# Rotating queries and keys from the raw projections, and normalising them afterwards in place

## The reference

```python
def attn_layer(x, Wqkv, qs, ksc, Wo):
    qkv = x @ Wqkv
    q, k, v = jnp.split(qkv, 3, -1)
    q, k, v = (sh(q), sh(k), sh(v))
    q = l2norm(q) * qs
    k = l2norm(k) * ksc
    q = q * cos * scale + rotate_half(q) * sin * scale
    inv = 1.0 / scale
    k = k * cos * inv + rotate_half(k) * sin * inv
    out = local_attention(q, k, v)
    ...
    return out @ Wo
...
for i in range(DEPTH):
    x = attn_layer(shift_tokens(x), Wqkv[i], q_scale[i], k_scale[i], Wo[i]) + x
    x = ffn_layer(shift_tokens(x), ln_g[i], ln_b[i], W1[i], b1[i], W2[i], b2[i]) + x
```

## Time and profile before

| | |
|---|---|
| median of 2 runs | 4887.01 us |
| the two runs | 4892.21 and 4881.81 us |
| span of the profiled execution | 4869.5 us |
| busy share of the span: TensorE, VectorE, ScalarE, GpSimd | 78%, 79%, 51%, 49% |
| wait of GpSimd for `QN` | 1791.2 us in 192 times |
| one layer (from one L1041 at 418.95 to the same at 804.53) | 385.6 us |

### The profile page before, as it was taken

One profiled execution on the slowest core, in us unless ns is written; L12 is line 12 of the kernel. 1 busy time (PEld: TensorE's weight loads), 2 busy tenths in 40 slices (PEclk: granted clock), 3 DMA queues, 4 the chain that ended last, 5 costly groups with the idle time before them and its releaser, 6 DMA issues.

```text
span 4869.5 us, 152986 instructions
## 1 busy us (share of the span) xinstructions
PE 3785.1 (78%) x64080; PEld 2581.5 (53%) x64080; DVE 3828.5 (79%) x6082; ACT 2483.4 (51%) x3705; POOL 2389.1 (49%) x1426
## 2 busy tenths in 40 slices
PE   5887887787787787788777877877877887887887
PEld 3554554554555455456435645554554554554554
DVE  4886886896896897797448878877976886986896
ACT  3554554554554565455225545554554554553553
POOL 3663563563664564455006535544553653553552
PEclk9998899899899999888878989999988998998999
DMA  2221221221221222122002212221221221221221
GB/s 82 54 57 46 53 55 48 53 54 44 58 56 51 49 57 58 40 55 63 6 10 51 57 47 51 56 57 43 57 58 39 55 59 40 57 55 44 53 57 46
DMA packets 179337, 247.34 MB, mean 51 GB/s; under 512 B 52516, under 2 KB 75040, under 8 KB 177184
## 3 DMA queue, kind: packets, MB, share of 16 engines
q1 hardware_dynamic: 178976, 242.09, 19.6%
HBM read 39.51 MB, written 1.05 MB: 8 GB/s over the span
## 4 chain that ended last, share of the span: by engine, by line
PE 35%; POOL 18%; DVE 17%; ACT 10%; issue 8%; DVEq 7%; SPq 3%; DMA 1%; ACTq 0%; POOLq 0%
POOL V L1185 9%; PE PS L390 6%; PE PS L544 5%; POOL V L1191 5%; POOL V L1193 5%; PE PS L382 4%; PE PS L466 3%; PE PS L416 3%; DVEq L1000 3%; DVE QN L927 3%; PE PS L383 2%; PE PS L384 2%; DVEq L921 2%; PE PS L576 2%; ACT PR L743 2%
## 5 line engine op out<-in xcount | busy, mean ns | idle before, releaser
L1185 POOL TENSOR_TENSOR V<-QN,TAB 128x512 f32<-128x512 f32 x768 | 1116.7, 1485 | 1791.2 <-DVE QN L927 1791.2
L382 PE MATMUL PS<-WH,XH 128*128 128x512 f32 x1152 | 634.4, 551 | 427.8 <-DVE XL L945 338.8
L697 ACT ACTIVATE RAWQK<-PS 128x1024 f32<-128x1024 f32 x384 | 392.3, 1022 | 848.5 <-PE PS L384 808.1
L934 DVE TENSOR_TENSOR U<-QN,TAB 128x1024 f32<-128x1024 f32 x384 | 736.8, 1922 | 16.4 <-issue 15.3
L390 PE MATMUL PS<-EYE,V 128*128 128x128 f32 x3072 | 449.6, 285 | 188.0 <-POOL V L1193 107.8
L1191 POOL TENSOR_TENSOR V<-V,U 128x1024 f32<-128x1024 f32 x192 | 516.6, 2690 | 81.3 <-DVE U L934 60.8
L382 PEld LDWEIGHTS PS<-WH,XH 128*128 128x128 f32 x1152 | 241.5, 210 | 560.4 <-DVE XL L945 210.3
L1193 POOL TENSOR_TENSOR V<-V,U 128x1024 f32<-128x1024 f32 x192 | 453.6, 2362 | 140.4 <-DVE U L934 140.4
L390 PEld LDWEIGHTS PS<-EYE,V 128*128 128x128 f32 x3072 | 366.1, 147 | 276.6 <-POOL V L1193 139.8
L384 PE MATMUL PS<-WL,XH 128*128 128x512 f32 x1152 | 511.2, 444 | 0.0
L383 PE MATMUL PS<-WH,XL 128*128 128x512 f32 x1152 | 511.0, 444 | 0.0
(11 more groups left out here) (150 smaller groups left out, 6509.1 us busy)
## 6 DMA issues: line engine op xcount, KB each, us to landing
V<-VS SPq DMA_DIRECT2D x3072, 64.0 KB, 2.0
U<-wqkv SPq DMA_DIRECT2D x13, 1024.0 KB, 5.2
V<-wqkv SPq DMA_DIRECT2D x13, 512.0 KB, 6.8
WO<-wo SPq DMA_DIRECT2D x13, 512.0 KB, 3.8
W<-w SPq DMA_DIRECT2D x12, 341.0 KB
ROT<-c_rot SPq DMA_DIRECT2D x1, 2048.0 KB, 10.4
QKS<-qks SPq DMA_DIRECT2D x13, 128.0 KB, 3.7
W<-w SPq DMA_DIRECT2D x12, 114.0 KB
```

The lines of the kernel that those rows point to most:

```text
L382: pe.matmul(o, XH[:, p, :], WH[:, w], start=True, stop=False)
L934: dve.tensor_tensor(paired(U[:, k]), split(QN[:, k]), per_dim(TAB[:, 2 * k * DH:(2 * k + 1) * DH], DH), ALU.mult).then_inc((u_q, u_k)[k], 1)
L1185: ins = pool.tensor_tensor(paired(V[:, k])[:, :, :, h * half:(h + 1) * half], split(QN[:, k])[:, :, :, (1 - h) * half:(2 - h) * half], per ...
```

## The change

The product with the reciprocal norm moves behind the rotation, which it commutes with. VectorE reads the raw projection straight from the PSUM banks `RAW` for its half (`rotate`), GpSimd reads ScalarE's copy `RAWQK` for its own. The sum is multiplied in place by the reciprocal norm on VectorE (`scale_rows`) in the next step. `QN` is gone; `V` has become a double buffer `VB`. TensorE projects the keys and values only after VectorE's read of the banks (`u_q`, `u_k` in place of `cp_q`, `cp_k`), and turns `VB` after the product (`nq_ready`, `nk_ready`).

```diff
 # TensorE
-                    pe.wait_ge(cp_q, c(1))
+                    pe.wait_ge(u_q, c(1))
                     project(1, p, 0)
...
-                    pe.wait_ge(rot_q, c(0))
-                    turn_qk(0, [0])
-                    pe.wait_ge(rot_ready, c(0))
-                    turn_qk(0, [1]).then_inc(t0_ready, 1)
+                    pe.wait_ge(nq_ready, c(0))
+                    turn_qk(0, q, [0])
+                    pe.wait_ge(nk_ready, c(0))
+                    turn_qk(0, q, [1]).then_inc(t0_ready, 1)
                 if a:
-                    pe.wait_ge(cp_k, c(1))
+                    pe.wait_ge(u_k, c(1))
                     project(2, p, 0).then_inc(raw_v0, 1)
 # ScalarE
-                        act.wait_ge(qn_ready, c(0))
+                        act.wait_ge(vv_ready, c(0))
                     raw(0, raw_q, cp_q, sq_q)
 # VectorE
-                if past(i, 1):
-                    dve.wait_ge(vv_ready, c(0))
-                for k in range(2):
-                    ins = dve.tensor_tensor(QN[:, k], RAWQK[:, k], rep(RN[:, k, :], [P, HEADS, DH], 2), ALU.mult)
-                ins.then_inc(qn_ready, 1)
+
+            def scale_rows(k, q, c):
+                dve.wait_ge((rot_q, rot_ready)[k], c(0))
+                rn = RN[:, k, :].rearrange("p (r j) -> p j r", r=2).unsqueeze(3).broadcast_to([P, NP_, 2, DH])
+                v = VB[:, q, k].rearrange("p (j r) d -> p j r d", r=2)
+                dve.tensor_tensor(v, v, rn, ALU.mult).then_inc((nq_ready, nk_ready)[k], 1)
+
+            def rotate(k, i, c):
+                if k == 0:
+                    dve.wait_ge(tab_ready, c(1))
                 if past(i, 1):
+                    dve.wait_ge((rot_q, rot_ready)[k], c(0))
+                dve.wait_ge((cp_q, cp_k)[k], c(1))
+                src = PS[:, RAW:RAW + 2, :].rearrange("p r (j d) -> p r j d", d=DH)
+                dve.tensor_tensor(paired(U[:, k]), src, per_dim(TAB[:, 2 * k * DH:(2 * k + 1) * DH], DH),
                                   ALU.mult).then_inc((u_q, u_k)[k], 1)
...
                 if b:
-                    rotate(1, None)
+                    scale_rows(0, 1 - p, c)
+                if a:
+                    rotate(0, i, c)
+                if b:
+                    scale_rows(1, 1 - p, c)
...
                 if a:
+                    rotate(1, i, c)
                     sum_squares(1)
...
-                if a:
-                    if past(i, 1):
-                        dve.wait_ge(rot_ready, c(0))
-                    rotate(0, c(1))
 # GpSimd
-                pool.wait_ge(qn_ready, c(1))
-                if past(i, 1):
-                    pool.wait_ge(t1_ready, c(0))
+                if past(i, 2):
+                    pool.wait_ge(t1_ready, c(-1))
                 half = DH // 2
                 for k in range(2):
+                    pool.wait_ge((cp_q, cp_k)[k], c(1))
                     for h in range(2):
```

More of the change, by code:

```diff
@@ L121, in build @@
         TAB = sb("TAB", [P, 4 * DH])
-        QN = sb("QN", [P, 2, HEADS, DH])
         U = sb("U", [P, 2, HEADS, DH])
-        V = sb("V", [P, 2, HEADS, DH])
+        VB = sb("VB", [P, 2, 2, HEADS, DH])
+        V = VB[:, 0]
         QT = sb("QT", [P, 2, NP_, P])
@@ L150, in build @@
         HT = ht_[:, 0:4 * GT].rearrange("p (i t) -> p i t", t=GT)
-        W_IN = [U[:, 0], U[:, 1], V[:, 0]]
+        W_IN = [U[:, 0], U[:, 1], VB[:, 0, 0]]
         W_IN = [w.rearrange("p a b -> p (a b)") for w in W_IN]
         DG4 = U[:, :, :, :].rearrange("p a b c -> p (a b c)").rearrange("p (g t) -> p g t", t=GT)
-        v_flat = V[:, :, :, :].rearrange("p a b c -> p (a b c)")
+        v_flat = VB[:, 0].rearrange("p a b c -> p (a b c)")
         D2M = v_flat[:, 0:2 * GT].rearrange("p (g t) -> p g t", t=GT)
@@ L159, in build @@
         HTM = (HT, DG4)
-        XIO = QN[:, :, :, :].rearrange("p a b c -> p (a b c)").rearrange("p (c d) -> p c d", d=P)
+        XIO = VB[:, 1].rearrange("p a b c -> p (a b c)").rearrange("p (c d) -> p c d", d=P)
         WQM = sb("WQM", [P, P])
@@ L394, in _, with turn_qk @@
             both = [(TQ + h // 4, h) for h in range(NP_)]
-            def turn_qk(g, parts=range(2)):
+            def turn_qk(g, q, parts):
                 for qk in parts:
-                    mm = turn(lambda h: V[:, qk, 2 * h:2 * h + 2, :].rearrange("p r d -> p (r d)"),
+                    mm = turn(lambda h: VB[:, q, qk, 2 * h:2 * h + 2, :].rearrange("p r d -> p (r d)"),
                               [(TQ + qk, 4 * g + j) for j in range(4)])
@@ L424, in step @@
                 if part is not None:
-                    pe.wait_ge((xs_ready, cp_q, cp_k)[part], c(1))
+                    pe.wait_ge((xs_ready, u_q, u_k)[part], c(1))
                     mm = project(part, p, 0)
@@ L486, in step @@
                     pe.wait_ge(tevq, c(0))
-                    turn_qk(1, [0])
+                    turn_qk(1, q, [0])
                     pe.wait_ge(tev0, c(0))
-                    turn_qk(1, [1]).then_inc(t1_ready, 1)
+                    turn_qk(1, q, [1]).then_inc(t1_ready, 1)
                     score(q, range(0, 2))
@@ L773, in norm_before @@
                     act.wait_ge(ffn_w, val(act, lay * (16 * F_DMAS) + (inv * DEPTH + 1) * 16 * F_DMAS))
-                    act.wait_ge(qn_ready, val(act, lay * CH + (inv * DEPTH + 1) * CH))
+                    act.wait_ge(vv_ready, val(act, lay * CH + (inv * DEPTH + 1) * CH))
                 else:
@@ L960, in step @@
                         normalise(i, c)
-                    else:
-                        dve.drain()
-                        rotate(0, c(1))
                     return
@@ L1177, in step @@
                 pool.wait_ge(tab_ready, c(1))
-                pool.wait_ge(qn_ready, c(1))
-                if past(i, 1):
-                    pool.wait_ge(t1_ready, c(0))
+                if past(i, 2):
+                    pool.wait_ge(t1_ready, c(-1))
                 half = DH // 2
                 for k in range(2):
+                    pool.wait_ge((cp_q, cp_k)[k], c(1))
                     for h in range(2):
                         t = TAB[:, (2 * k + 1) * DH + h * half:(2 * k + 1) * DH + (h + 1) * half]
-                        ins = pool.tensor_tensor(paired(V[:, k])[:, :, :, h * half:(h + 1) * half],
-                                                 split(QN[:, k])[:, :, :, (1 - h) * half:(2 - h) * half],
+                        ins = pool.tensor_tensor(paired(VB[:, p, k])[:, :, :, h * half:(h + 1) * half],
+                                                 split(RAWQK[:, k])[:, :, :, (1 - h) * half:(2 - h) * half],
                                                  per_dim(t, half), ALU.mult)
@@ L1190, in step @@
                 pool.wait_ge(vv_ready, c(1))
-                pool.tensor_tensor(V[:, 0], V[:, 0], U[:, 0], ALU.add).then_inc(rot_q, 1)
+                pool.tensor_tensor(VB[:, p, 0], VB[:, p, 0], U[:, 0], ALU.add).then_inc(rot_q, 1)
                 pool.wait_ge(u_k, c(1))
-                pool.tensor_tensor(V[:, 1], V[:, 1], U[:, 1], ALU.add).then_inc(rot_ready, 1)
+                pool.tensor_tensor(VB[:, p, 1], VB[:, p, 1], U[:, 1], ALU.add).then_inc(rot_ready, 1)
             def ffn(inv, lay, start_next):
```

7 lines of the change are left out of this document (1 added, 6 removed).

## The result

The changed kernel takes **5591.74 us** (median of 2 runs, 5590.73 to 5592.75), 1.1447 times the kernel before (95% interval 1.1412 to 1.1481). The forecast was 5410 (5110 to 5590). Slower was right, but the loss is 705 us where 523 were worked out, and the time lies 1.7 us above the range. The profiled execution has a span of 5590.9, which is 721.4 more than the earlier trace rows.

A forecast was written before the change was run, and what follows sets the result against it. Bound: a cycle of ON, VectorE's list down to XL, query projection and weighing, neither engine full. 12 x (12 x 3.8 + 3.0 + 0.5 - 5.5) = +523 us on 4887 gives 5410 us, range 5110 to 5590.

The forecast's parts named there:

- The walk: One attention step from ON to the next ON, instruction by instruction: +3.8 us a step, ends +2.5 to +4.7.
- The clock: Lower TensorE clock level at the query projection to weighing: 4.03 us instead of 2.65, next ON at 23.3 instead of 22.0.
- the stretch of 3.01: TensorE from key projection to end of scores, 3.01 us; 0.9 more at the lower clock level, only in the upper end.
- VectorE's idle time before ON near 3 us: Sign expected in the new profile: VectorE idle near 3 us before ON in each step.
- The start of the layer: Steps 1 and 2, no ON: QN and POOL's run off TensorE's way, -5.5 us a layer, ends -8 and -2.
- The end of the layer: Interval 15 to 16, key chain but no XL: +3.0 us; step 16, S_q and S_k before the maximum: +0.5.
- The FFN: Chunk 0's projections wait for U with other work around them: costed at nothing, at most 1 us a layer.
- U freed from POOL: VectorE's U, with a PSUM input, no longer waits out POOL's instructions: 307 us less busy time in all.
- slower clock: Rival: both TensorE stretches at the lower level, 24.2 us a step, 3 us won at layer start: 5570 us; chance 0.19.
- Less contention: Rival: about half of the 4.1 us a step lost to POOL is not lost, step 21.3: 5120 us; chance 0.15.
- faster: Rival: VectorE sets the pace, U sheds its 307 us, everything else is covered: 4580 us; chance 0.04.
- No change: Rival: four long VectorE instructions for four, waits hidden: 4887 us; chance 0.07.

The follow-up runs named there:

- The wait alone: Kernel before, with TensorE's key projection also waiting for u_k, the second instruction after ON in VectorE's queue: 5450.3 us, ratio 1.1164.
- the kernel with both gaps filled: Changed kernel with extra unread TensorE products, fourteen ahead of the wait for U of the queries, six ahead of the wait for XL: 5314.7 us, ratio 1.0883.
- as XL did: Kernel before with VectorE's XL of the next chunk placed between its two QN products instead of behind both: 5320.8 us, ratio 1.0887.

## Why the prediction was right in kind and short in size

- **The place of the loss: right, and shown.** "TensorE's key projection at 4.2 instead of 0.45": it is at 4.23. The wait alone, put into the kernel before, costs 567 us, its share of the lower clock included.
- **The walk: right at the upper level.** It gave 22.0 at a granted clock of 1.00; the kernel with both gaps filled has 22.05, with its parts within 0.5 us of the walk. In the changed kernel itself the scores come later by the clock, and so do the norm (+14.66, not 12.35) and POOL's work on the keys (+10.0, not 8.2). They meet a little less: the norm loses 2.8 us to POOL and not 3.45 (5.5 from 737.50 to the end of its last instruction at 743.00, less its own 2.73).
- **The clock: the failed step.** "Query projection to the end of weighing ... one of 0.59 ... the next ON starts at 22.0 or 23.3": I took the lower level there, as in the kernel before, for 1.3 us, and only as an end "if the stretch of 3.01 also falls to the lower level, which I put at 0.9 more". It is the other way round: the price on the query projection was not paid, and the one on the stretch behind U, taken only in the upper end, was paid in every step. The query projection to the end of weighing has the upper level (743.94 to 746.57, 2.63 us), and the stretch of 3.01 has the lower one nearly throughout, for 5.24: +2.23, not +0.9. In the twelve steps of both kernels the lower level, where it comes, sits behind TensorE's longest wait, and the change moved that wait from XL to U. 22.0 + 2.23 less 0.65 for the norm is 23.6, against 23.87 in the step shown. Taken over a layer the step was forecast 0.51 too short, which is the 1.8 that the filled gaps give back less the 1.3 in the forecast: 12 x 12 x 0.51 = 73 us. The sign "VectorE's idle time before ON near 3 us" failed with it: it is 1.41, as the query projection is fast.
- **The start of the layer: the largest error beside the clock.** "I take -5.5, with -8 and -2 as ends": it is -0.74, outside the ends, 12 x 4.8 = 57 us. I had counted QN and the waits for V as won and had put no added wait there. The waits for V are gone, and 8.85 of the layer's 15.4 us stood in this stretch, where I had put the smaller part. But waits of the same length came in their place: the timelines of this stretch list 16.9 us of idle time before TensorE's instructions (those over 0.7 us) in the kernel before and 16.9 after it. TensorE now waits for U, and for an XL that the held-up norm delays: the norm of step 1 meets both of POOL's additions and lasts 7.35 us, where it lasted 5.67. VectorE also stands idle (put down to "issue") right before the S behind which U is queued; in the kernel before the same kind of idle time stood before a U that TensorE had no need of. First a row of the kernel before, then the changed kernel (start, duration, idle time before it):

```profile
459.45 1.12 PE L390 MATMUL PS<-EYE,V 128*128 128x128 f32 x4 [4.20 <-POOL V L1191]
...
517.23 1.23 DVE L929 TENSOR_TENSOR VB<-VB,RN 128x1024 f32<-128x1024 f32 x1 [2.49 <-issue]
...
519.64 0.80 PE L382 MATMUL PS<-WH,XH 128*128 128x512 f32 x1 [6.03 <-DVE U L939]
...
534.30 0.79 PE L382 MATMUL PS<-WH,XH 128*128 128x512 f32 x1 [5.32 <-DVE XL L950]
```

- **The end of the layer: mis-sized.** "Interval 15 to 16 ... +3.0" and "step 16 +0.5": +5.96, -2.91 and +2.46 for the three intervals, +5.5 where +3.5 stood; 24 us. Most of the first is the clock again: from the key projection (846.41) to the end of the scores (851.66) that interval has 5.25 us where the walk has 3.01.
- **The FFN:** taken at nothing, "at most 1 us a layer"; it is +0.64, 8 us. With the 36 by which the other layers exceed this one's 57.1, and 17 less outside the span than the two runs before had, the four terms make up the 182 us between forecast and result.
- **U freed from POOL: right in kind.** 1.21 without spread, 271 us less busy time against the 307 by median and shortest. What that is worth in time no run shows by itself; S and the norm lost more than it to POOL.
- **The rivals.** The mechanism of *slower clock* is the one that came, with 5570 by its sum and a chance of 0.19, against 5591.7. I put both stretches at the lower level; one was, at more than twice its price, so that its 5570 comes so near is in part luck. *Less contention* fell because 3.5 of the 4.1 us are lost (0.7 at S, 2.8 in the norm), and *faster* fell with the wait. *No change* fell too: the count of long VectorE instructions stayed at four, and TensorE's wait is not hidden. The Trainium skill's advice for chained VectorE operations, to minimise their count and not the semaphores (VectorE: DVE Perf Modes, Rules for kernel authors), does not cover this case: one wait more on TensorE, with no operation added or removed, costs 567 us.
- **The rule on GpSimd.** The Trainium skill (GPSIMD Engine Reference, Key points) has it that GpSimd gets in the way of VectorE instructions with two SBUF inputs or in a two-port mode. The trace agrees on U, which was 1.96 by its median and is 1.21, and on S (1.90 beside POOL, 1.21 without).

## What to carry to other kernels

Before an operand is moved from a copy to the PSUM bank itself, ask who waits for the bank: the reader then stands between TensorE and its next product, with everything that its own queue has before it, and that price is paid even if the reader gets faster. Walk the new step at the upper level first, then find TensorE's longest wait in the new order and price the lower level behind that one; in these runs that was the place, though not in every step when the wait was near 2 us. An instruction moved up in a queue takes its own wait along, as XL did.
